# One attention kernel on one core: the context of two key-value groups in one visit, in one PSUM bank of 512 columns

## What is computed

```python
def _lora_linear(x, W, A, B):
    return x @ W + SCALING * (x @ A @ B)
...
q = _lora_linear(hidden_states, Wq, Aq, Bq)   # 1024 columns, 32 heads
k = _lora_linear(traces, Wk, Ak, Bk)          # 256 columns, 8 heads
v = _lora_linear(traces, Wv, Av, Bv)
...
scores = jnp.einsum('bhqd,bhtd->bhqt', q, k) / jnp.sqrt(HD)
attn = jax.nn.softmax(scores, axis=-1)
context = jnp.einsum('bhqt,bhtd->bhqd', attn, v)
...
out = _lora_linear(context, Wo, Ao, Bo)
return hidden_states + out
```

## Time and profile before

| what | value |
|---|---|
| median of three executions | 755.97 us |
| span of the profiled execution | 753.1 us |
| its own time | not listed apart; the median is 2.9 us above the span |
| TensorE matmuls busy | 737.6 us, 98% |
| VectorE busy | 469.0 us, 62% |
| ScalarE busy | 382.0 us, 51% |
| GpSimd busy | 349.1 us, 46% |
| share of the chain that ended last | PE 88%, DVE 5%, DMA 2%, issue 2%, POOL 1% |
| mean granted TensorE clock | 0.998 |

### The profile page before, as it was taken

One profiled execution on the slowest core, in us unless ns is written; L12 is line 12 of the kernel. 1 busy time (PEld: TensorE's weight loads), 2 busy tenths in 40 slices (PEclk: granted clock), 3 DMA queues, 4 the chain that ended last, 5 costly groups with the idle time before them and its releaser, 6 DMA issues.

```text
span 753.1 us, 17856 instructions
## 1 busy us (share of the span) xinstructions
PE 737.6 (98%) x5776; PEld 645.2 (86%) x5776; DVE 469.0 (62%) x988; ACT 382.0 (51%) x1287; POOL 349.1 (46%) x322
## 2 busy tenths in 40 slices
PE   7899999999999999999999999999999999999998
PEld 6678899889989989999998998999867788888886
DVE  5957687687768668767876866787696412212211
ACT  4437665666666666666666666665685210111100
POOL 4757645745654574565557457555766100000000
PEclk9999999999999999999999999999999999999999
DMA  7775544554453555345454544645464834343331
GB/s 257 271 219 164 169 140 140 159 172 122 139 174 126 157 152 163 119 139 175 138 156 149 155 131 128 172 139 178 139 181 154 276 130 156 117 167 111 111 111 56
DMA packets 94665, 117.01 MB, mean 155 GB/s; under 512 B 8624, under 2 KB 76208, under 8 KB 94640
## 3 DMA queue, kind: packets, MB, share of 16 engines
q1 hardware_dynamic: 94640, 116.69, 49.3%
HBM read 78.91 MB, written 37.75 MB: 155 GB/s over the span
## 4 chain that ended last, share of the span: by engine, by line
PE 88%; DVE 5%; DMA 2%; issue 2%; POOL 1%; ACT 0%; SPq 0%; POOLq 0%; DVEq 0%
PE banks L868 32%; PE banks L917 23%; PE banks L897 15%; PE banks L906 8%; PE banks L882 7%; DVE neg_max L718 2%; PE banks L853 2%; DVE x_lo L725 2%; DMA probs_t<-wq 1%; PE banks L855 1%; DMA probs<-b4q 1%; DMA probs_t<-b4kv 1%; POOL k_stack L510 1%; DVE lora L679 0%; DVE probs_t L263 0%
## 5 line engine op out<-in xcount | busy, mean ns | idle before, releaser
L525 POOL TENSOR_TENSOR probs<-probs,rsums 128x512 f32<-128x512 f32 x256 | 266.4, 1041 | 205.4 <-DVE rsums L750 204.6
L582 ACT ACTIVATE probs<-banks,neg_max 128x256 f32<-128x256 f32 x512 | 238.7, 475 | 175.7 <-DVE neg_max L718 170.8
L718 DVE TENSOR_REDUCE neg_max<-banks 128x2 f32<-128x512 f32 x256 | 174.3, 682 | 20.0 <-PE banks L882 20.0
L897 PE MATMUL banks<-ident,probs 128*128 128x128 f32 x1024 | 157.1, 276 | 2.2 <-POOL probs L525 2.0
L263 DVE COPY probs_t<-banks 128x512 f32<-128x512 f32 x192 | 132.4, 690 | 43.0 <-PE banks L897 35.6
L868 PE MATMUL banks<-x_hi,w_hi 128*128 128x256 f32 x512 | 145.7, 285 | 0.8 <-POOL w_lo L500 0.4
L868 PE MATMUL banks<-x_hi,w_lo 128*128 128x256 f32 x512 | 144.6, 282 | 0.0
L868 PE MATMUL banks<-x_lo,w_hi 128*128 128x256 f32 x512 | 144.5, 282 | 0.0
L897 PEld LDWEIGHTS banks<-ident,probs 128*128 128x128 f32 x1024 | 115.5, 140 | 30.8 <-issue 27.1
L882 PE MATMUL banks<-k_stack,q_stack 96*128 96x256 f32 x512 | 122.8, 322 | 0.0
L582 ACT ACTIVATION_READ_ACCUMULATOR probs<-banks,neg_max 128x1 f32 x512 | 104.0, 203 | 0.0
(11 more groups left out here) (76 smaller groups left out, 1112.9 us busy)
## 6 DMA issues: line engine op xcount, KB each, us to landing
q_stack<-q_parts SPq DMA_DIRECT2D x192, 128.0 KB, 2.5
q_parts<-q_stage SPq DMA_DIRECT2D x64, 256.0 KB, 2.2
raw<-ct SPq DMA_DIRECT2D x32, 256.0 KB, 3.9
raw<-xt SPq DMA_DIRECT2D x32, 256.0 KB, 4.4
context<-ctx_stage SPq DMA_DIRECT2D x64, 128.0 KB, 1.8
probs<-xn SPq DMA_DIRECT2D x16, 512.0 KB, 4.1
out<-raw SPq DMA_DIRECT2D x15, 512.0 KB, 2.9
probs_t<-context SPq DMA_DIRECT2D x7, 1024.0 KB, 5.9
```

Of the source, the lines that this page charges most:

```text
L525: nc.gpsimd.tensor_tensor(probs[:, c], probs[:, c], rsums[:, c, :].unsqueeze(2).broadcast_to([P, 2, S]), ALU.mult).then_inc(norm_done, 1)
L582: last = nc.scalar.activation(probs[:, c, h, :], score_bank[c][:, S * h:S * (h + 1)], ACT.Exp, bias=neg_max[:, c, h:h + 1], scale=-1.0, ac ...
L718: nc.vector.tensor_reduce(out=neg_max[:, c, :], in_=score_bank[c].rearrange("p (h t) -> p h t", h=2), axis=AXIS, op=ALU.min).then_inc(max_ ...
L897: last = nc.tensor.transpose(bank[:, P * (2 * t + h):P * (2 * t + h + 1)], probs[:, c, h, P * t:P * (t + 1)], ident[:])
```

## The change

The context of two units is computed in one visit, at c = 0 of every other unit (slots 8, 16, 24 and 32), in one PSUM bank of 512 columns: 16 matmuls, 32 instructions. `probs_t` holds four units (16 KB more in each partition), and the space reserved for descriptors of DMAs, `dynamic_dma_scratch_size`, is set to 1024 bytes. VectorE copies 128x512 once where it copied 128x256 twice. The banks turn with a period of nine users per pair of units. SyncE stores both contexts of a pair one after the other, after the pair is done, so its queue is in another order.

```diff
-        probs_t = sb("probs_t", [P, 2, 2, GH, S], F32)
+        probs_t = sb("probs_t", [P, 4, 2, GH, S], F32)
...
-            return turn_bank[(5 * unit + (0, 2, 3, 4)[c]) % 2]
+            return turn_bank[(9 * (unit // 2) + ((0, 2, 3, 4), (5, 6, 7, 8))[unit % 2][c]) % 2]
+
+        def ctx_bank(pair):
+
+            return turn_bank[(9 * (pair + 1) + 1) % 2]
...
                 stack_q(3, fills + 2, score0 + 8)
-                store_ctx(0)
                 send(pos["q", 4, 0])
                 stack_q(4, fills + 3, score0 + 12)
                 send(pos["q", 5, 0])
+                store_ctx(0)
                 store_ctx(1)
...
-                    for g, loads in ((3, 2), (None, 2), (4, 1), (5, 3), (6, 2), (7, 2)):
+                    for g, loads in ((2, 0), (3, 2), (None, 2), (4, 4), (5, 0), (6, 4), (7, 0)):
...
                         if g == 6:
-                            wait(ctx_mm, NB * NG - 1)
+                            wait(ctx_mm, NB * NG - 2)
...
-                if c == 1 and not prologue:
-                    u = unit - 1
-                    dve.wait_ge(ctx_mm, b * NG + (u + 1))
-                    dve.wait_ge(ctx_stored[u % 2], b * (4 * DMA) + DMA * (u // 2 + 1))
-                    nc.vector.tensor_copy(ctx_stage[:, u % 2, :],
-                                          turn_bank[(5 * unit + 1) % 2][:, 0:S]).then_inc(ctx_done, 1)
+                if c == 1 and unit % 2 == 0 and not prologue:
+                    pair = unit // 2 - 1
+                    dve.wait_ge(ctx_mm, b * NG + 2 * (pair + 1))
+                    for i in range(2):
+                        dve.wait_ge(ctx_stored[i], b * (4 * DMA) + DMA * (pair + 1))
+                    nc.vector.tensor_copy(ctx_stage[:].rearrange("p u q -> p (u q)"),
+                                          ctx_bank(pair)).then_inc(ctx_done, 2)
...
+            def context(pair):
+
+                for i in range(2):
+                    unit = 2 * pair + i
+                    for t in range(2):
+                        for h in range(GH):
+                            last = nc.tensor.matmul(
+                                ctx_bank(pair)[HD * h:HD * (h + 1), S * i:S * (i + 1)],
+                                v_sb[:, t, HD * (unit % NG):HD * (unit % NG + 1)],
+                                probs_t[:, unit % 4, t, h, :], start=(t == 0), stop=(t == 1),
+                                tile_position=(0, HD * h))
+                last.then_inc(ctx_mm, 2)
...
-                    if c == 2 and not prologue:
+                    if c == 2 and unit % 2 == 0 and not prologue:
                         pe.wait_ge(ctx_done, b * NG + unit)
+                    if c == 1 and unit % 2 == 1:
+                        pe.wait_ge(pt_act, b * NG + unit)
...
-                if c == 0:
+                if c == 0 and unit % 2 == 0:
                     u = unit - 1
...
-                    context(u)
+                    context(u // 2)
...
+    nc = bacc.Bacc("TRN2", target_bir_lowering=False, num_devices=1,
+                   dynamic_dma_scratch_size=1024)
```

More of the change, by code:

```diff
@@ L256, in turn_of @@
         def turn_of(unit, c):
-            return turn_bank[(5 * unit + (0, 2, 3, 4)[c]) % 2]
+            return turn_bank[(9 * (unit // 2) + ((0, 2, 3, 4), (5, 6, 7, 8))[unit % 2][c]) % 2]
+        def ctx_bank(pair):
+            return turn_bank[(9 * (pair + 1) + 1) % 2]
         def copy_turned(op, unit, c):
-            dst = probs_t[:, unit % 2, :, 2 * (c % 2):2 * (c % 2) + 2, P * (c // 2):P * (c // 2 + 1)]
+            dst = probs_t[:, unit % 4, :, 2 * (c % 2):2 * (c % 2) + 2, P * (c // 2):P * (c // 2 + 1)]
             src = turn_of(unit, c).rearrange("p (t h q) -> p t h q", t=2, h=2)
@@ L405, in body @@
                     stack_k(0, b + 2, score0 + 16)
-                store_ctx(2)
                 send(pos["q", 6, 0])
@@ L424, in body @@
                     return
+                store_ctx(2)
                 store_ctx(3)
@@ L428, in body @@
                 send(pos["k", 1, 1])
-                store_ctx(4)
                 send(pos["q", 0, 1])
                 stack_q(0, fills + 5, score0 + 28)
+                store_ctx(4)
                 store_ctx(5)
@@ L436, in body @@
                 send(pos["q", 2, 1])
-                store_ctx(6)
                 send(pos["q", 3, 1])
                 stack_q(2, fills + 6, score0 + 36)
+                store_ctx(6)
                 store_ctx(7)
@@ L1011, in slot @@
                     pe.wait_ge(pt_dve, b * (3 * NG) + 3 * (u + 1))
-                    if u == 0:
+                    if u == 1:
                         pe.wait_ge(proj_out, b * PER + PRO)
-                    context(u)
+                    context(u // 2)
             for s in range(FIRST):
@@ L1077 @@
     arrays = {n: np.ascontiguousarray(a) for n, a in arrays.items()}
-    nc = bacc.Bacc("TRN2", target_bir_lowering=False, num_devices=1)
+    nc = bacc.Bacc("TRN2", target_bir_lowering=False, num_devices=1,
+                   dynamic_dma_scratch_size=1024)
     args = [nc.dram_tensor(n, a.shape, mybir.dt.from_np(a.dtype), kind="ExternalInput").ap()
```

## The result

The changed kernel takes 760.21 us (median of 15 executions, 757.85 to 764.65); the kernel before, run beside it, 756.17 (15 executions, 753.8 to 760.3). The ratio is 1.0059, 95% interval 1.0041 to 1.0077: 3.1 to 5.8 us slower. The forecast of 756.9 (no change) missed; the range of 751.0 to 762.0 held the time.

The account below looks back on a forecast made before the run. The prediction took TensorE to bound the kernel. Its terms (-9.5 + 6.0 + 3.8 + 0.5 - 0.5 + 0.6) summed to +0.9 on a span of 753.1, plus 2.9 to the median: 756.9 us, range 751.0 to 762.0.

Parts of the forecast that it names:

- Term 1: TensorE's context visits: 64 become 32, each saving 0.30 us of entry and exit; -9.5 us.
- Term 2: Slots 17 to 21: without slot 20's visit TensorE waits for VectorE's x_lo burst, 0.86 us in seven batches; +6.0 us.
- term 3: Slot 16: unit 5's restacked q loses 1.77 us of slack on SyncE's queue, so TensorE waits; +3.8 us.
- Term 4: Last batch: unit 7's q has 0.63 us slack and loses slot 20's visit of 1.16; +0.5 us.
- 5, low part at the end: End of the slots: the longer last visit covers TensorE's wait for the last low part of output weights; -0.5 us.
- term 6: Output projection: batch 1's context load now waits behind unit 6's store, so TensorE waits; +0.6 us.
- rival 1: Slower: restacked q later than in the profile; 759.8 us at 0.5 later per batch, near 763 at 1.0; chance 0.28.
- At nothing: VectorE's copy saving of 0.15 us per pair, ScalarE's copy wait and GpSimd's low parts of c were counted as zero.
- The offset: The median stands 2.9 us above the profiled span of 753.1; the forecast kept that difference.
- the likeliest case: The forecast itself: no change, 756.9 us, own range 754.5 to 758.2; chance 0.42.
- Rival 3: Faster: nothing is late, with terms 2, 3, 4 and 6 zero; 746.0 us; chance 0.05.
- Rival 2: Faster: VectorE less late, its third x_lo quarter no longer overlapping GpSimd's multiplication; 753.5 us, or 751.3 with good q landings; chance 0.20.

Follow-up runs that it names:

- e5: The changed kernel with one projection matmul of the same slot issued between the two units of a visit (29 of 32 visits broken); 770.0 us.
- e7: The changed kernel with VectorE's waits for the stores ahead of its wait for the context matmuls, before the 512-column copy; 759.5 us.
- e9: As e8, but only units (0,1) and (6,7) merged, units 2 to 5 visited singly, last batch's weight loads in another order; 752.07 us.
- e2: The changed kernel with unit 5's q restacked ahead of the four loads on SyncE's queue; 757.44 us.
- e3: The changed kernel with the third quarter of x_lo computed on GpSimd instead of VectorE; 759.35 us.
- e4: The changed kernel, last batch only: unit 7's q ahead of two weight loads, batch 1's context load ahead of unit 6's store; 759.9 us.
- e1: The kernel before with only the change's memory side: probs_t four units deep and 1024 bytes of descriptor space; 756.85 us.
- e8: The changed kernel with the edits of e2, e4 and e7 and the third quarter of x_lo in slot 18; 752.81 us.
- e6: The kernel before with the third quarter of x_lo computed in slot 18, ahead of the reciprocal, instead of slot 19; 754.55 us.
- e10: As e9, with four sends of q (units 6, 7, next batch's 0 and 1) each ahead of a context store; 748.49 us.
- e11: The kernel of e8 unchanged, run again beside e10 on the same chip; 752.34 us.

## Why the prediction was right or wrong, point by point

| term | forecast | measured | how |
|---|---|---|---|
| 1, visits | -9.5 | -8.6 | 32 x 0.27, from the stretches without a wait |
| 2, `x_lo` | +6.0 | +7.1 | 7 x (0.74 + 0.27), see below |
| 3, unit 5's q | +3.8 | +2.6 to 6.6 | lengthening of slot 16, five profiled executions, mean 4.1 |
| 4, last batch | +0.5 | +1.05 | slot 21, but by another wait |
| 5, low part at the end | -0.5 | -0.5 | the wait is gone |
| 6, batch 1's context | +0.6 | +0.5 | the wait at L923 |

The sum of the measured column, with 4.1 for term 3, is +3.65, against 4.0 by the medians and an interval from 3.1 to 5.8. With the 2.6 of after's own profile it is 2.15, against 2.6 between the two profiled spans from slot 3 on. (Term 2: slots 17 to 24 hold one pair and should have shrunk by 0.27; they grew by 0.87 - 0.13 = 0.74 instead, 1.01 a batch.)

**Term 1** was right in mechanism, which e5 shows directly. The size was off by 0.03 a pair. The prediction set the entry and exit at 0.30 from the waves (its 32 x 0.30 is 9.6, not 9.5); the trace gives 0.27 for a pair saved, e5 0.33 for a pair broken.

**Term 2** failed in one step: "The copy starts after 0.14", taken over from the copy of one unit. Behind it the working held to 0.02 us (9.84 against 9.86). The copy now had one more wait queued in front of it, and started 0.32 behind its slot: 7 x 0.18 = 1.3 us. e7 shows that the order of these waits is worth 0.11 of the 0.18. What the other 0.07 is stays open; it goes with the pair, for in e9, which has both kinds with the store waits first, the copy of one unit starts 0.14 behind its slot and that of a pair 0.21.

**Term 3** was right in place and about right in size, and e2 shows it: with unit 5's q ahead of the loads the waits are gone and 2.8 us come back. What the forecast did not hold was the scatter. The slot is lengthened, in the five profiled executions that have this order (after, e3, e4, e5, e7), by 2.6, 3.2, 6.6, 5.1 and 3.2 in sum. The waits alone sum to 1.8, 2.1, 3.5, 3.0 and 2.1. The prediction's sign of being wrong spoke of the waits, under 2 or over 6: by it term 3 fails in after's own profile, on the low side, and holds in the other four. The large ones come from the last batch, where a wait of 1.48 (e4) or 2.36 (e5) was followed by a lower clock and cost 3.3 and 4.2. This is rival 1 in part: not q later in each batch, but a long wait that costs about twice its length. How much of the term is the lost visit and how much the added store, 1.16 and 0.61 in the forecast, no run separates.

**Term 4** named the wrong step. It put the loss of slot 20's visit in the last batch at unit 7's q, with slack 0.63. That q landed at 566.07, 0.44 ahead of its scores at 566.51; the fold in slot 21 waited for `w_lo`. e4 moved the q and the wait stayed; e9 has a visit at slot 20 and it is gone. The lost visit was the right cause, the resource was not: the prediction looked along SyncE's queue and not along the chain of ScalarE's `w_hi` and VectorE's `w_lo`. Whether q would have been late had the scores not been 1.05 later themselves stays open.

**Terms 5 and 6** held. **At nothing:** these costs stayed at nothing.

**The offset.** "The median stands 2.9 above that span, and I keep that" was wrong in kind: the device time stands 1.8 above the span in each profiled execution, so the profiled execution of before took about 754.9, 1.3 less than the median of 15. One part of it is the start. Slot 3 begins at 64.40 there and at 67.11 in after; but e1, which has no edit of TensorE's work, has 67.06, and the other kernels lie between 64.3 (e4) and 66.75 (e8). Of these 2.7 us, 1.6 are the granted clock: slots 0 to 2 take 3.38 to 3.40 in before, e2, e4, e7, e8 and e9, where it stays at 2.4 GHz, and 4.60 to 4.96 in after, e1, e3, e5, e6, e10 and e11, where it stands at 1.2 GHz for some 3 us, beginning between 61.2 and 63.7 us. Both groups have kernels of each kind, so these 2.7 of the 5.3 us between the two spans are scatter of the start, not the change. By luck the offset led to a base of 756.0, next to the median of 756.17, and cost the forecast nothing.

So of the 3.1 us between forecast and result (+0.9 and +4.0), term 1 makes 0.9, term 2 1.1, term 4 0.55 and term 3 0.3; term 6 gives 0.1 back, and 0.35 is left, well inside the interval. This split takes the mean of five executions for term 3 and is no sharper than that mean. No single rival came true; the likeliest case lost through four sizes, all on the same side, and the range held since it was wide enough for their sum.

**Rival 3** fell with terms 2 and 3, whose waits came. **Rival 2** described a real price: e6 gets 0.32 a batch back in the kernel before by removing the overlap of VectorE's third quarter and GpSimd's multiplication, and in e8, with e7's order, slots 17 to 21 fall by 0.58. The change did not move it by itself, as the prediction argued.

Where did the gain of 8.6 us go? 7.1 went into VectorE's burst of `x_lo`, since the visit that used to give VectorE time at slot 20 was one of those merged away, and 3 to 4 into unit 5's q, which lost the time of slot 12's visit and got one more store ahead of it. e9 and e10 turn this round: they keep the four visits at slots 12 to 24 and merge only two pairs. A loop batch then takes 64.69 instead of e8's 64.91, and slot 21 of the last batch is 1.05 shorter. These 2.6 us show in the traces, but the medians of e9 and e8 are only 0.7 apart, and e10, the fastest, has its sends moved as well.

## What to carry to other kernels

Work that is taken off the bounding engine also takes away the time in which the others caught up: list, for every place where an instruction group disappears, which engine or queue was late there, and walk along each of them, not only the one that comes to mind. Merge where nothing follows in a hurry, keep the visits where a burst is due. In a loop, queue the wait that ends last behind those long fulfilled. Putting sends that somebody will wait for ahead of stores that nobody waits for went with 3.6 us here, by a cause that the runs leave open.

## What the runs showed of the hardware

- VectorE's subtraction of two SBUF operands (128x512) takes 0.68 us alone, 1.17 beside GpSimd's multiplication and 1.19 in another slot (e3); the neighbour, not the place, sets it (e6).
- In the loop, two fulfilled waits queued behind the last one delay VectorE's copy by 0.11 us (0.32 against 0.21, e7); in the written-out last batch they do not (0.19 against 0.23).
- Behind four waits of TensorE for q, of 1.48 (e4), 2.28 (e9), 2.36 (e5) and 3.15 us (e11), the granted clock fell to its lower level, 1.2 GHz, for some 3 us; behind those of 0.63, 0.92 (after), 1.20 (e7) and 1.37 (e3) it stayed at 2.4 GHz. The slot then grew by 4.06 for a wait of 2.28, and by 3.33 for one of 1.48. The length of the wait alone does not decide it: ahead of slot 0 TensorE waits 1.70 us for GpSimd in before, e1, e4, e7 and e10, and the clock then fell in e1 and e10 only.
- Fifteen executions of the changed kernel spread over 6.8 us, and the mean granted clock goes with that: the five at 0.993 have spans of 759.6 to 762.8 us, the five at 0.998 and above 756.0 to 758.4. One profiled execution can stand 4.4 us from the median of its kernel (e11: 756.69 against 752.34).
